# Attention in query halves, with paired projections through DRAM and GpSimd taking part in the low parts

## The reference

```python
x = layer_norm(x, ln_m_g, ln_m_b)              # the context, 6404 rows
lat = layer_norm(latents, ln_l_g, ln_l_b)      # the 1024 tokens
q = lat @ Wq
kv = jnp.concatenate([x, lat], axis=1) @ Wkv   # 7428 keys
k, v = jnp.split(kv, 2, axis=-1)               # 16 heads of 64
dots = jnp.einsum('bhid,bhjd->bhij', q, k) * 64 ** -0.5
out = jnp.einsum('bhij,bhjd->bhid', jax.nn.softmax(dots, axis=-1), v)
return out.reshape(b, m, heads * dim_head) @ Wout
```

## Time and profile before

| | |
|---|---|
| median of 3 runs | 2882.32 us (2880.21 to 2882.97) |
| span of the profiled execution | 2884.0 us |
| PE, busy | 2658.8 us, 92% |
| DVE, busy | 2348.5 us, 81% |
| ACT, busy | 2271.1 us, 79% |
| POOL, busy | 55.4 us, 2% |
| bytes by DMA | 22.30 MB |

### The profile page before, as it was taken

The page is one execution under the profiler, slowest core; times in us unless marked ns, Lnnn a source line. Parts: engine busy times, 40 slices in busy tenths (PEclk is TensorE's granted clock), DMA queues, the critical chain, the costliest instruction groups (busy, mean ns, idle before and its releaser), DMA issues. The chain is left out here.

```text
span 2884.0 us, 93692 instructions
## 1 busy us (share of the span) xinstructions
PE 2658.8 (92%) x35639; PEld 1734.1 (60%) x35639; DVE 2348.5 (81%) x3328; ACT 2271.1 (79%) x2645; POOL 55.4 (2%) x95
## 2 busy tenths in 40 slices
PE   2799999999999999999999999999999999959996
PEld 1256665656565656565656566666656566747884
DVE  8789897979797979798888888888979797547864
ACT  4889897979797979797979798988979795426652
POOL 2100000000000000000000000000000000012001
PEclk9999999999999999999999999999999999979998
DMA  2000000000000000000000000000000000060000
GB/s 75 1 2 1 2 1 2 1 2 1 2 1 1 1 1 1 1 2 1 2 1 2 1 2 0 2 1 2 1 2 0 2 1 2 8 169 1 2 2 10
DMA packets 16345, 22.30 MB, mean 8 GB/s; under 512 B 1960, under 2 KB 13808, under 8 KB 15728
## 3 DMA queue, kind: packets, MB, share of 16 engines
q1 hardware_dynamic: 12816, 14.55, 1.7%
q10 hardware_dynamic: 3296, 4.10, 0.5%
HBM read 18.13 MB, written 0.52 MB: 6 GB/s over the span
## 5 line engine op out<-in xcount | busy, mean ns | idle before, releaser
L800 DVE TENSOR_TENSOR att_prob_low<-att_prob 128x1024 f16<-128x1024 f32 (+1 forms) x944 | 1153.7, 1223 | 196.7 <-ACT att_prob L678 195.9
L678 ACT ACTIVATE att_prob<-all_banks 128x1024 f32<-128x1024 f32 (+1 forms) x944 | 966.0, 1025 | 112.8 <-PE all_banks L565 32.6
L672 ACT ACTIVATE att_scores<-all_banks 128x1024 bf16<-128x1024 f32 x768 | 783.2, 1024 | 0.9 <-PE all_banks L495 0.6
L553 PEld LDWEIGHTS all_banks<-att_v,att_prob 128*128 128x128 bf16 x7552 | 538.3, 99 | 117.5 <-issue 16.1
L553 PE MATMUL all_banks<-att_v,att_prob 128*128 (+1 forms) x7552 | 597.7, 193 | 5.1 <-ACT att_prob L678 5.1
L554 PE MATMUL all_banks<-att_v,att_prob 128*128 (+1 forms) x7552 | 598.5, 195 | 0.0
L554 PEld LDWEIGHTS all_banks<-att_v,att_prob 128*128 128x128 bf16 x7552 | 506.0, 98 | 101.6
L535 PE MATMUL all_banks<-att_qc,att_kc 128*128 (+1 forms) x1888 | 562.5, 379 | 0.0
L535 PE MATMUL all_banks<-att_qd,att_kd 128*128 (+1 forms) x1888 | 562.0, 379 | 0.0
L495 PE MATMUL all_banks<-att_kc,att_qc 128*128 (+1 forms) x1792 | 534.3, 380 | 19.0 <-ACT att_scores L672 14.2
L774 DVE TENSOR_TENSOR att_running<-att_running,att_scores 128x1024 bf16<-128x1024 bf16 x768 | 525.9, 685 | 13.9 <-ACT att_scores L672 13.5
(11 more groups left out here) (276 smaller groups left out, 2810.3 us busy)
## 6 DMA issues: line engine op xcount, KB each, us to landing
prep_ctx<-in_ctx SPq DMA_DIRECT2D x5, 640.0 KB, 8.6
later_ctx<-in_ctx SPq DMA_DIRECT2D x1, 3200.0 KB
experts_up<-in_L_ffn_f SPq DMA_DIRECT2D x1, 2048.0 KB, 8.3
prep_wkv<-in_L_xattn_Wkv ACTq DMA_DIRECT2D x1, 1024.0 KB, 12.3
all_X<-in_x SPq DMA_DIRECT2D x1, 512.0 KB, 4.5
prep_wq<-in_L_xattn_Wq ACTq DMA_DIRECT2D x1, 512.0 KB, 14.5
wout_w<-in_L_xattn_Wout SPq DMA_DIRECT2D x1, 512.0 KB, 4.1
out<-all_X SPq DMA_DIRECT2D x2, 256.0 KB, 2.5
```

What stands on the lines that cost most here:

```text
L553: pe.matmul(O[:, j // 4, o:o + DH + 1], w, high, start=False, stop=False, skip_group_check=True)
L672: act.activation(o[:, :], banks[:, :, :].rearrange("p a q -> p (a q)"), ACT.Copy).then_inc(max_copied, 1)
L678: act.activation(prob[t % 2][0:n, :], S[t % 2][0:n, :], ACT.Exp, scale=SCALE).then_inc(exp_done, 1)
L800: dve.tensor_tensor(prob_low[t % 2][0:n, :], p, p.bitcast(BF16)[:, 1:2 * TOKENS:2], op=ALU.subtract)\
```

## The change

The two passes over a key tile's 1024 queries become two halves of 512 queries, each over all keys. A unit is now two key tiles for 512 queries (`HALF`, `PAIRS`, 60 units per head, the 30th and the 60th of the four last keys alone), so a result needs one PSUM bank O and not two. Three buffers prob and three prob_low take the place of two each.

The bank that this frees, Y, takes the projections: a task (one chunk of K or Q for two heads at once on 128 partitions, or four tiles of V for two heads) is put on PE in every third unit (`side_task`), copied by ACT, subtracted by DVE in the unit behind, and written by SP from two staging buffers to DRAM. Even heads project K and Q of the next pair, odd heads its V. SP loads a head's K, Q and V from DRAM, K and Q twice for the two halves of the partitions, into one of two sets of buffers, at the start of the head before (V for even heads near its end). The weights are no longer doubled in `stage_prepare`.

The maxima are taken by DVE straight from PSUM, 120 chunks per head in a ring of two banks X, two chunks per unit, without copies by ACT and without a running maximum. They run 24 units off the head's start (`OFFSET`). The spread is made in two halves, in units 26 and 56.

POOL subtracts the low parts in 44 of 60 units (`by_pool`), DVE in units with g % 4 = 1 and in the two tail units. The loop now holds two heads and runs seven times; heads 14 and 15 stand behind it. Inner loops are gone.

```diff
+HALF = TOKENS // 2
+PAIRS = FULL_TILES // 2
+UNITS = 2 * (PAIRS + 1)
...
+        NP, NL = 3, 3
+        prob = [sc.sb(f"prob{n}", [P, 2 * BANK]) for n in range(NP)]
+        prob_low = [sc.sb(f"prob_low{n}", [P, 2 * BANK], F16) for n in range(NL)]
+        NR = 2
+        stage_h = [sc.sb(f"stage_h{n}", [P, BANK], F16) for n in range(NR)]
...
-        X = pers.banks[:, 4:6, :]
-        O = pers.banks[:, 6:8, :]
+        X = [pers.banks[:, 4 + n, :] for n in range(2)]
+        Y = pers.banks[:, 6, :]
+        O = pers.banks[:, 7, 0:4 * (DH + 1)]
...
+        def by_pool(g):
+            return g % 4 != 1 and g % SIDE != PAIRS
...
+        def slots_at(b, e, g):
+
+            n = 2 * ((g - OFFSET) % UNITS)
+            return (b, e, n) if g < OFFSET else (b + 1, 1 - e, n)
...
+            def load_kq(m):
+                e = m % 2
+                sp.dma_start(kc[0:DH, e, :], k_high[rows(m), :]).then_inc(k_in[e], 16)
+                sp.dma_start(kc[DH:P, e, :], k_high[rows(m), :]).then_inc(k_in[e], 16)
+                sp.dma_start(qc[0:DH, e, :], q_high[rows(m), :]).then_inc(q_in[e], 16)
+                sp.dma_start(qc[DH:P, e, :], q_low[rows(m), :]).then_inc(q_in[e], 16)
+                sp.dma_start(qd[0:DH, e, :], q_high[rows(m), :]).then_inc(q_in[e], 16)
+                sp.dma_start(kd[0:DH, e, :], k_low[rows(m), :]).then_inc(k_in[e], 16)
...
+                for g in range(UNITS):
+                    if by_pool(g):
+                        pool.wait_ge(exp_done, EXP0 + b * UNITS + g + 1)
+                        pool.wait_ge(low_done, LOW0 + b * UNITS + g - 2)
+                        p = prob[g % NP][:, :]
+                        pool.tensor_tensor(prob_low[g % NL][:, :], p, p.bitcast(BF16)[:, 1:4 * BANK:2],
+                                           op=ALU.subtract).then_inc(split_pool, 1)
...
+            def max_slot(m, e, n, turn):
+
+                j, c = divmod(n, K_CHUNKS)
+                if n == 0:
+                    pe.wait_ge(q_in[e], 48 * (turn + 1))
+                    pe.wait_ge(k_in[e], 48 * (turn + 1))
+                pe.wait_ge(max_taken, 2 + m * SLOTS + n - 1)
+                pe.matmul(X[n % 2][:, 0:kwidth(c)], qc[:, e, j * P:(j + 1) * P],
+                          kc[:, e, c * BANK:c * BANK + kwidth(c)], start=True, stop=True).then_inc(max_scored, 1)
...
+                for g in range(UNITS):
+                    p = g % SIDE
+                    m, me, n = slots_at(b, e, g)
+                    slots = with_max or m is b
+                    if p:
+                        apply_high(b, e, g, i)
+                    if slots:
+                        max_slot(m, me, n, i if m is b else i + e)
+                    if p >= 2:
+                        apply_low(b, e, g - 2)
+                    side_task(b, e, g, with_max, projecting, i)
+                    if slots:
+                        max_slot(m, me, n + 1, i if m is b else i + e)
+                    next_score(b, e, g, with_max)
...
+            def exp(b, g):
+                act.wait_ge(scored, b * UNITS + g + 1)
+                act.wait_ge(high_done, HIGH0 + b * UNITS + g - 2)
+                wait_split(act, *((b, g - 3) if g >= 3 else (b - 1, g - 3 + UNITS)))
...
+                    if g + 1 < UNITS:
+                        exp(b, g + 1)
+                    elif with_max:
+                        exp(b + 1, 0)
+                    n = task_at(e, g) if projecting else None
+                    if n is not None:
+                        copy_task(i + 1, n)
...
+            def take(m, n):
+                j, c = divmod(n, K_CHUNKS)
+                dve.wait_ge(max_scored, m * SLOTS + n + 1)
+                dve.tensor_reduce(part[:, j, c:c + 1], X[n % 2][:, 0:kwidth(c)], axis=AX.X, op=ALU.max)\
+                   .then_inc(max_taken, 1)
...
+                    if slots:
+                        take(m, n)
+                    t = task_at(e, g - 1) if projecting and g else None
+                    if t is not None:
+                        split_task(i + 1, t)
+                    if not by_pool(g):
+                        split(b, g)
+                    if slots:
+                        take(m, n + 1)
```

More of the change, by code:

```diff
@@ L351, in stage_attention @@
+        zeros = sc.sb("zeros", [P, 4 * (DH + 1)], F16)
         warm = sc.sb("warm", [1, 1])
-        S = [pers.banks[:, 2 * n:2 * n + 2, :].rearrange("p b q -> p (b q)") for n in range(2)]
-        X = pers.banks[:, 4:6, :]
-        O = pers.banks[:, 6:8, :]
[L355 to L359, removed]
@@ L372, in kwidth @@
             return min(BANK, KEYS - c * BANK)
[L374 to L407, removed]
@@ L418, in _ @@
+            with pool.Fori(0, HEADS) as b:
+                head(b)
         @block.tensor
         def _(pe):
[L420 to L435, removed]
@@ new lines, in apply_low @@
+            def apply_low(b, e, g):
+                wait_split(pe, b, g)
+                for i, t in tiles(g):
+                    for q in range(4):
+                        w = prob_low[g % NL][:, i * BANK + q * P:i * BANK + (q + 1) * P]
+                        o = q * (DH + 1)
+                        last = pe.matmul(O[:, o:o + DH + 1], w, v[:, e, t, 0:DH + 1], start=False, stop=True,
+                                         skip_group_check=True)
+                last.then_inc(low_done, 1)
@@ new lines, in next_score, with head @@
+            def next_score(b, e, g, with_max):
+                if g + 2 < UNITS:
+                    score(b, e, g + 2)
+                elif with_max:
+                    score(b + 1, 1 - e, g + 2 - UNITS)
+            def head(b, e, with_max, projecting, i):
+                for g in range(UNITS):
+                    p = g % SIDE
+                    m, me, n = slots_at(b, e, g)
[10 more added lines that the diff above has]
+                    next_score(b, e, g, with_max)
+                    if p == 0:
+                        apply_high(b, e, g, i)
+                    if p == PAIRS:
+                        apply_low(b, e, g - 1)
+                        apply_low(b, e, g)
@@ new lines, in head @@
+            def head(b, e, with_max, projecting, i):
+                for g in range(UNITS):
+                    if g + 1 < UNITS:
+                        exp(b, g + 1)
+                    elif with_max:
+                        exp(b + 1, 0)
+                    n = task_at(e, g) if projecting else None
+                    if n is not None:
+                        copy_task(i + 1, n)
+                    elif g == BACK_AT:
+                        place_top(b, e, 1)
+                    elif g == FRONT_AT and with_max:
+                        place_top(b + 1, 1 - e, 0)
@@ new lines, in _ @@
+            act.wait_ge(constants, 1)
+            act.activation(warm[:, :], zeros[0:1, 0:1], ACT.Exp).then_inc(exp_done, EXP0)
+            for n in range(KQ_TASKS):
+                if n >= NF:
+                    act.wait_ge(first_out[n % NF], 32 * (n // NF))
+                copy_kq(0, n, pers.banks[:, n % 4, :], FIRST_H[n % NF])
+            act.wait_ge(filled, 3)
+            for n in range(KQ_TASKS, TASKS):
+                copy_v(0, n, pers.banks[:, n % 4, :])
+            place_top(0, 0, 0)
@@ new lines, in _ @@
+            for n in range(KQ_TASKS):
+                split_kq(0, n, pers.banks[:, n % 4, :], FIRST_H[n % NF], FIRST_L[n % NF])
+            for n in range(KQ_TASKS, TASKS):
+                split_v(0, n, pers.banks[:, n % 4, :])
+                for x in FIRST_SLOTS[n - KQ_TASKS]:
+                    take(0, x)
+                    if x + 1 == SLOTS // 2:
+                        finish_max(0, 0)
+            with dve.Fori(0, HEADS // 2 - 1) as it:
+                head(2 * it, 0, True, True, it)
+                head(2 * it + 1, 1, True, True, it)
```

727 lines of the change are left out of this document (327 added, 400 removed).

## The result

The changed kernel takes 3102.8 us (median of 4 runs, 3101.62 to 3107.81) against 2882.64 us for the kernel before on the same chip (4 runs): 1.077 times as long, 95% interval 1.0754 to 1.0785. It is slower by 220 us. The profiled execution has a span of 3101.9 us and a mean granted clock of 0.962.

What follows compares the result with a forecast made beforehand. PE, 92% busy, was taken to bound the kernel. Start 167, 14 heads of 131.6 + 27.3 stalls, 48.0 jumps, head 14 and 128.2 for head 15 ended attention at 2720.6, +222.1: 3104 us, range 2830 to 3330.

Steps and rivals of the forecast that it cites:

- PE's floor per head, 131.6: Attention head on PE without stalls: 58 units of 2.03 us plus tails, spread and projections, 131.6 us instead of 149.2.
- Who is first, by 0.17 us: In units with g%4 = 1, POOL's subtraction starts 0.17 us before DVE asks, so DVE's probability split is held.
- The stalls, 27.3 us per projecting head: PE's waits for maxima behind 14 held DVE splits, summed to 27.3 us in each head with projections.
- The terms of 2.31 and 1.67: PE loss per held split: 2.31 us, or 1.67 where a nearby projection task hides 0.64.
- Reductions pass freely: DVE's maximum reductions from PSUM stay at 0.69 us beside POOL's subtractions, not held.
- The jump, 3.6 + 4.4 = 8.0: Each of six outer-loop jumps back costs a 3.6 us PE pause plus 4.4 of slow clock, 48 in all.
- DMA at nothing: SP's queue of head loads and staged writes was taken to cost no time.
- the bound of 6: Other bound for DMA: staged writes behind the loads in SP's queue cost 6 us per pair of heads, 42 us.
- Start and last head: Head 0 starts at 167 us (155 to 190); head 15 takes 128.2, its last 34 units at 1.85 each.
- A: Rival: DVE asks before POOL, stalls are 11.7 us per head, 2848 us in all; chance 0.16.
- B: Rival: DVE is never held for large instructions, stalls 5.5 us per head, 2756 us; chance 0.12.
- C: Rival: PE's pauses drop the clock, 4.4 us per fall; 3174 us at one per head, up to 3597; chance 0.12.

Runs made afterwards that it cites:

- e8: The changed kernel with DVE's subtraction ahead of the unit's first maximum and the next head's loads spread over the third to eleventh unit: 2698.8 us, 0.937 of the kernel before.
- e3: The changed kernel with DVE taking all subtractions of low parts and POOL none: 3009.8 us, 1.045 times the kernel before.
- e4: The changed kernel with the next head's loads issued in the ninth unit of a head, not the first: 3103.4 us, 1.077 times the kernel before.
- e5: The changed kernel with the next head's loads issued in the third unit of a head, not the first: 3097.5 us, 1.075 times the kernel before.
- e1: The changed kernel with DVE's large subtraction placed ahead of the unit's first maximum, not behind it: 2748.0 us, 0.954 of the kernel before.
- e6: The changed kernel with DVE subtracting ahead of the first maximum and the loads in the third unit: 2767.2 us, 0.960 of the kernel before.
- e2: The changed kernel with POOL taking all large subtractions, DVE only those of the tail units: 2753.9 us, 0.956 of the kernel before.
- e7: The changed kernel with each large POOL subtraction written as two of 128x512: 2916.0 us, 1.012 times the kernel before.

## Why the prediction was right, point by point

It forecast 3104 us by held subtractions, and 3102.8 came. The total is that close because errors cancel; by part, from the zero products of the heads and the rows above:

| term | forecast | measured |
|---|---|---|
| head 0 begins | 167 | 179.9 |
| 14 heads and 6 jumps | 2272.6 | 2274.0 |
| head 14 | 152.8 | 150.3 |
| head 15 | 128.2 | 117.6 |
| end of the attention | 2720.6 | 2721.8 |
| what lies behind it | 385.5 | 380.1 |

*PE's floor per head, 131.6.* Measured 133.2, from e8, where PE has no gap. The unit is 2.03 us as forecast: in e8 most units without a task are 2.03 or 2.04. The 1.6 too few are in what comes on top; which part stays open.

*Who is first, by 0.17 us.* Measured 0.15. The margin on which the sign of the whole change hung was there, and it didn't drift: 148 of the 224 large subtractions of DVE take 2.8 us, and 43, of which 42 stand behind a projection's split and so ask later, 2.2.

*The stalls, 27.3 us per projecting head.* Measured about 24: the head from 833.82 to 989.95 is 22.9 longer than the floor, and two heads with one jump average 326.0, less 2 x 133.2 and 11.7 at the jump. The terms of 2.31 and 1.67 were 1.86 and 1.2 for most. The hold was shorter, as POOL's instruction takes 1.89 and not the 2.12 of the earlier trace rows, and DVE needs only 1.09 after its release, not 1.22. The step "who waits behind the held instruction" held.

*Reductions pass freely.* In the changed kernel the 1358 large reductions that run beside a POOL subtraction average 684 ns, and so do the 434 that don't; e3 has 683. The forecast from another instruction of the earlier trace rows was right.

*The jump, 3.6 + 4.4 = 8.0.* Wrong in both terms. The pause was 9.2 to 9.8, since a head's loads now go out at that moment; e4 and e5 show it by taking them away. The clock's part was smaller than 4.4: 2.6 to 6.0 us at half speed behind the six jumps instead of 8.9, so 2.2 us of work on average. Together 11.7 against 8.0. Over the 14 heads the floor was 22 us too short, the jumps 22, and the stalls 43 too long: that these cancel to 1.4 us is luck.

*DMA at nothing.* Right for the writes in the changed kernel (one wait of 7.1 us), but, it seems, only because PE paused at the six jumps while the loads ran. What wasn't seen is that the loads meet the jump. The mechanism that was named as the bound, a stage write behind the loads, is real: moving the loads by two units brings it out, at 6 to 7 us per pair, near the bound of 6.

The Trainium skill, "DMA: Bandwidth & Descriptors", section "Queues, rings and completion order", says that each DMA engine consumes the descriptors of a ring in order. The trace agrees: with the write behind all eight loads ACT waited 44.3 us in all in e5, with one to three ahead of it none in e8.

*Start and last head.* The start was 13 us too early. Of the 83.8 to 105.1 in which PE waits for K and Q, the forecast had the end at 97; the other 5 lie in the twelve tasks and the V load. Head 15 was 10.6 too long, and here a step was wrong: its last 34 units, which have no maxima, were taken to be bound by the shared access at 1.85 us each. They take 1.60, which is PE's own 2.03 less the 0.43 of two maxima. Window and DVE timeline of the changed kernel:

```profile
2676.00:2716.00 40.00, 40.00 (x701) 28.18 (x700) 14.47 (x7) 25.61 (x25) 37.82 (x20) 1.00 0.01 2
...
2690.03 2.30 DVE L810 TENSOR_TENSOR att_prob_low<-att_prob 128x1024 f16<-128x1024 f32 x1 [4.24 <-ACT att_prob L734]
```

DVE is held as before (2.30 us), but no reduction stands behind it, and PE is busy for all 40 us: a hold costs by what waits behind it. That is 34 x 0.25 = 8.5 of the 10.6 us, and the six smaller stalls are the rest. The part behind the attention is 5.4 us shorter than in the kernel before. All of it lies in the last expert stage; up to that the two kernels agree within 0.3 us, and the cause stays open.

*The rivals.* A (DVE asks first, 2848) and B (never held, 2756) didn't happen. e1 shows that making DVE ask first is worth more than A gave, because A's sum kept the subtraction behind the first maximum, where five units in a head were still held. C had a small part. In the head of 833.82 to 989.95 the granted clock is 1.00 with all its pauses, but the ten falls in other heads came right behind waits of about 2 us like the one at 460.01. Each is 3.4 us long; a head without the jump takes 158.2 us with a fall and 156.1 without. So C cost some 2 us a fall, by estimate about 20 in all, and not the 70 or more of its sum. These are within the stalls above.

## What to carry to other kernels

When work goes from VectorE to GpSimd, look in the trace at who asks first for the two tiles that both read from SBUF, and put VectorE's instruction where GpSimd's isn't ready yet; 0.15 us decided 355. Count what is queued behind the instruction that may be held, and if the order can't be changed, make GpSimd's instructions shorter. Loads of the next stage belong neither on a loop's jump back nor in one block ahead of small writes for which an engine waits: in portions between the writes, e8 shows no wait for them.

## What the runs showed of the hardware that was not expected

A pause of PE at a jump back depends on what the DMA queues carry: 3.3 to 3.9 us without loads (e4, e5, e6, e8), 8.5 to 9.9 beside 5.1 MB of them (the changed kernel, e1, e2, e3, e7), with a body of two heads each time; the kernel before has 3.4 to 3.9 with a body of one. That it is the fetch of instructions is likely, as nothing else is waited for, but no row shows the fetch itself.

How long the clock stays at 1.2 GHz behind a jump isn't set by the pause alone, nor by the code behind it. In the kernel before it is 8.9 us, in the changed kernel 2.6 to 6.0. In e8 the same code runs behind all six jumps, after pauses of 3.3 to 3.8 us. Windows behind two of them, the pauses being 3.76 and 3.50:

```profile
722.70:728.60 5.90, 5.90 (x43) 3.42 (x44) 2.52 (x3) 1.62 (x2) 0.69 (x1) 0.50 0.02 4
...
996.60:1003.00 6.40, 6.40 (x83) 3.98 (x84) 5.40 (x8) 2.65 (x3) 2.59 (x2) 1.00 0.13 45
```

Behind the second the clock didn't fall at all. What decides stays open.

A waiting VectorE gets the access as soon as GpSimd's instruction ends, even when GpSimd has its next one ready (e7). In these traces no hold of DVE lasts more than one instruction of POOL.
